# x's parts of two gates put into PSUM by ScalarE, update gate's products side by side in all steps

## The reference, cut to what matters

```python
vz = video @ C_z + b_z      # vr, vh likewise
xz = jnp.einsum('btd,de->bte', seq, W_z)   # xr, xh likewise
def step(h, xs):
    xzt, xrt, xht = xs
    z = jax.nn.sigmoid(xzt + h @ U_z + vz)
    r = jax.nn.sigmoid(xrt + h @ U_r + vr)
    hh = jnp.tanh(xht + r * h @ U + vh)
    h_new = (1.0 - z) * h + z * hh
    return (h_new, h_new)
```

## Time and profile before

| | |
|---|---|
| median of three runs | 1515.9 us |
| span of the profiled execution | 1513.4 us |
| the profiled execution's own time | not given; the median is 2.5 us above its span |
| TensorE busy | 1503.4 us, 99% |
| VectorE busy | 1332.9 us, 88% |
| ScalarE busy | 1066.1 us, 70% |
| GpSimd busy | 309.1 us, 20% |
| granted TensorE clock | 1.000 in the mean over the span |
| recurrence, t = 1 to the last product | 551 to 1508 us |

### The profile page before, as it was taken

How to read it: one execution, slowest core, us unless ns; L and a number is a source line. 1 busy time by engine, 2 the same in 40 slices (tenths; PEclk the granted TensorE clock), 3 DMA queues, 4 the chain that set the end, 5 groups by cost and what they waited for, 6 DMA issues and landing times.

```text
span 1513.4 us, 58048 instructions
## 1 busy us (share of the span) xinstructions
PE 1503.4 (99%) x24698; PEld 1177.8 (78%) x24698; DVE 1332.9 (88%) x2928; ACT 1066.1 (70%) x2481; POOL 309.1 (20%) x333
## 2 busy tenths in 40 slices
PE   9999999999999999999999999999999999999998
PEld 7874444444444467779999999999999999999998
DVE  7999999999999889888888888888888888877787
ACT  7989999999999833656666666566666666656333
POOL 1100112111110014322222222222222222222222
PEclk9999999999999999999999999999999999999999
DMA  5156465565649978533333333333333333320000
GB/s 198 35 158 189 94 194 139 136 157 145 176 89 143 148 112 82 74 51 23 49 21 49 48 21 49 45 24 49 21 48 47 20 48 30 39 41 4 31 32 31
DMA packets 544979, 116.86 MB, mean 77 GB/s; under 512 B 520144, under 2 KB 527056, under 8 KB 536016
## 3 DMA queue, kind: packets, MB, share of 16 engines
q1 hardware_dynamic: 537424, 82.21, 31.2%
q0 software_dynamic: 7008, 30.41, 10.9%
q10 hardware_dynamic: 288, 0.52, 0.1%
HBM read 66.47 MB, written 33.55 MB: 66 GB/s over the span
## 4 chain that ended last, share of the span: by engine, by line
PE 97%; DVE 2%; issue 1%; ACT 1%; DMA 0%; DVEq 0%
PE ps L1458 33%; PE ps L1560 22%; PE ps L1523 22%; PE ps L1572 12%; PE ps L1544 5%; PE ps L1476 2%; DVE ST L1303 0%; PE ps L1425 0%; DMA AR<-in_w1f 0%; PE ps L1489 0%; DVE RL L1338 0%; DVE AR L1270 0%; DVE HL L1382 0%; DVE ST L1308 0%; DVE ST L1389 0%
## 5 line engine op out<-in xcount | busy, mean ns | idle before, releaser
L1458 PE MATMUL ps<-XH,WH 128*128 128x512 f16 x1872 | 404.7, 379 | 0.0
L1458 PEld LDWEIGHTS ps<-XH,WH 128*128 128x128 f16 x1872 | 182.9, 98 | 220.2 <-issue 0.3
L1560 PE MATMUL ps<-HL,U 128*128 128x64 f16 x8016 | 275.5, 193 | 2.0 <-DVE HL L1382 1.7
L1560 PEld LDWEIGHTS ps<-HL,U 128*128 128x128 f16 x8016 | 259.2, 98 | 8.5 <-issue 3.5
L1675 POOL TENSOR_TENSOR ST<-ST 128x256 f32<-128x256 f32 x127 | 107.9, 849 | 460.5 <-ACT ST L869 460.5
L847 ACT ACTIVATE ST<-ST 128x128 f32<-128x128 f32 x254 | 71.9, 310 | 169.5 <-DVE ST L1303 169.5
L1572 PE MATMUL ps<-HL,U 128*128 128x64 f16 x4064 | 163.2, 194 | 0.0
L1303 DVE SCALAR_TENSOR_TENSOR ST<-ps,dn,AR 128x128 f32<-128x128 f32 (+1 forms) x320 | 108.6, 372 | 46.8 <-PE ps L1572 44.2
L1303 DVE SCALAR_TENSOR_TENSOR ST<-ps,dn,XP 128x128 f32<-128x128 f32 x315 | 107.4, 372 | 41.2 <-PE ps L1572 38.9
L1572 PEld LDWEIGHTS ps<-HL,U 128*128 128x128 f16 x4064 | 138.6, 98 | 0.1
L1560 PEld LDWEIGHTS ps<-RL,U 128*128 128x128 f16 x3952 | 131.9, 98 | 6.0 <-issue 0.9
(11 more groups left out here) (201 smaller groups left out, 2976.4 us busy)
## 6 DMA issues: line engine op xcount, KB each, us to landing
x_scratch<-AR SPq DMA_DIRECT2D x16, 1024.0 KB, 5.3
AR<-in_x POOLq DMA_DIRECT2D x15, 1024.0 KB, 8.1
AR<-HB POOLq DMA_DIRECT2D x11, 1024.0 KB, 7.0
raw<-x_scratch SPq DMA_DIRECT2D x88, 128.0 KB, 4.5
out_y<-raw SPq DMA_DIRECT2D x11, 1024.0 KB, 4.6
raw<-in_x SPq DMA_DIRECT2D x10, 1024.0 KB, 7.4
ST<-in_x SPq DMA_DIRECT2D x5, 1024.0 KB, 7.3
out_y<-AR SPq DMA_DIRECT2D x4, 1024.0 KB, 4.3
```

Of the source, the lines that this page charges most:

```text
L1458: op = pe.matmul(ps[b][:, :], v[:, g, wp, k, e * P:(e + 1) * P], y[:, xp, k, :], start=n == 0, stop=n == 11)
L1560: pe.matmul(ps[b][:, col:col + B], U[:, g, uh, k, e * P:(e + 1) * P], S[:, k, 0], start=opens, stop=False, skip_group_check=True)
```

## The change

It does three things.

1. **Two gates get x's part ahead of their products.** `held(t, g)` is true for R in steps 2 to 127 and for C in steps 2 to 119. In such a step ScalarE has put x's part, times a factor (`uh`), into the gate's two banks with one instruction (`put_x`, 256 elements), before the gate's first product; that product then doesn't open the bank anew but adds to what is there. VectorE's `add_x` falls away, and ScalarE's sigmoid and tanh read the bank, with the factor `dn` as their scale. R's put for step t+1 stands in ScalarE's program behind the f16 copy of r*h in step t; C's stands at the end of step t, behind the splitting of later x. TensorE waits for the puts (`s_put`) where it waited for the adds. In the first eight steps of C this also ends its being joint.
2. **Z is joint in all steps.** `is_joint` is `g == 0`. VectorE's add for Z is then two instructions, the second waiting for the first.
3. Three one-column factors `uh` are computed by VectorE in step 0; the eight banks are one tensor, so that one instruction can write two of them. Some semaphores are merged.

```diff
-JOINT = TC
+HELD_FROM, HELD_TO = 2, 15 * 8
...
         def is_joint(t, g):
-            return g != 1 and t < JOINT
+            return g == 0
+
+        def held(t, g):
+            return g == 1 and t >= HELD_FROM or g == 2 and HELD_FROM <= t < HELD_TO
...
+            def put_x(t, g):
+                j, tt = divmod(t, TC)
...
+                else:
+                    act.wait_ge(s_xp, xp_ready(t, g))
+                    if by_seven(j):
+                        act.wait_ge(s_xa, xa_count[turn(j, g, 4)])
...
+                    act.wait_ge(s_r if g == 1 else s_hh, 2 * (t - 1) + (0 if g == 1 else 2))
+                first = (R if g == 1 else C)[0]
+                banks = PS[:, first * 512:(first + 2) * 512].rearrange("p (h n) -> p h n", h=2)[:, :, 0:2 * B]
+                x = XP[j % 2][:, g].rearrange("p (h e) n -> p h e n", h=2)[:, :, :, tt * B:(tt + 1) * B]
+                act.activation(banks.rearrange("p h (e b) -> p h e b", e=2), x, ACT.Copy, scale=uh[:, g:g + 1]).then_inc(s_put[g], 1)
...
                     for h in range(2):
-                        act.wait_ge(s_pr, 2 * u + h + 1)
-                        act.activation(two(rg, h), two(rg, h), ACT.Sigmoid).then_inc(s_r, 1)
+                        if held(t, 1):
+                            act.wait_ge(s_R, 2 * u + h + 1)
+                            act.activation(two(rg, h), held_sums(R[h]), ACT.Sigmoid, scale=dn[:, scale(4)]).then_inc(s_r, 1)
...
+                    if t + 1 < T and held(t + 1, 1):
+                        put_x(t + 1, 1)
...
+                if t and t + 1 < T and held(t + 1, 2):
+                    put_x(t + 1, 2)
...
-                for h in range(2):
+                for h in range(0 if held(t, 1) else 2):
                     dve.wait_ge(s_R, 2 * u + h + 1)
                     add_x(t, rg, R[h], 1, (2 * h, 2 * h + 1), None, s_pr, 2 * u + h + 1)
...
-                                opens = kk == 0 and k == 0 and uh == int(joint) and (e % 2 == 0 if banks[0] != banks[1] else e == 0)
+                                opens = not held(t, g) and kk == 0 and k == 0 and half == int(joint) and (e % 2 == 0 if banks[0] != banks[1] else e == 0)
...
-                else:
-                    pe.wait_ge(s_pr, 2 * u)
+                elif held(t, 1):
+                    pe.wait_ge(s_put[1], puts(t, 1))
...
-                if u:
-                    pe.wait_ge(s_pc, 2 * u)
+                if held(t, 2):
+                    pe.wait_ge(s_put[2], puts(t, 2))
+                elif u:
+                    pe.wait_ge(s_hh, 2 * t)
```

More of the change, by code:

```diff
@@ L120, in build @@
         hhi, hlo, rhi, rlo = HL[:, :, 0], HL[:, :, 1], RL[:, :, 0], RL[:, :, 1]
-        ps = [ctx.enter_context(nc.psum_tensor(f"ps{i}", [P, 512], F32)) for i in range(8)]
+        PS = ctx.enter_context(nc.psum_tensor("ps", [P, 8 * 512], F32))[:, :]
+        ps = [PS[:, i * 512:(i + 1) * 512] for i in range(8)]
         W1F, W1I, W1H, UZ, UR, UH, CR, CZ, WR, WZ, CH, WH = range(12)
@@ L246, in build @@
         s_R, s_Z, s_C = sem("R"), sem("Z"), sem("C")
-        s_pr, s_zh, s_pz, s_ch, s_pc = (sem(n) for n in ("prer_", "z_high", "prez_", "c_high", "preh_"))
+        s_put = {1: sem("x_in_R"), 2: sem("x_in_C")}
+        s_pr, s_zh, s_pz, s_pc = (sem(n) for n in ("prer_", "z_high", "prez_", "preh_"))
         s_r, s_rhi, s_rf, s_rlo = (sem(n) for n in ("r", "rhi", "rf_", "rlo"))
@@ L387, in is_joint, with puts, sums_by_dve @@
         def is_joint(t, g):
-            return g != 1 and t < JOINT
+            return g == 0
+        def held(t, g):
+            return g == 1 and t >= HELD_FROM or g == 2 and HELD_FROM <= t < HELD_TO
+        def puts(t, g):
+            return sum(held(n, g) for n in range(t + 1))
+        def sums_by_dve(t, g):
+            return sum(not held(n, g) for n in range(1, t + 1))
         def halved_by_act(t):
@@ L731, in put_dv @@
                 put(i, DV[:, turns[i][1]], s_predv)
+            def put_x(t, g):
+                j, tt = divmod(t, TC)
+                if puts(t, g) == 1:
+                    act.wait_ge(s_ux1, 4)
+                if j == 0:
+                    act.wait_ge(s_xpa, KT * (W2_ORDER.index(g) + 1))
+                    act.wait_ge(s_xpb, KT * (B_ORDER.index(g) + 1))
+                else:
+                    act.wait_ge(s_xp, xp_ready(t, g))
+                    if by_seven(j):
+                        act.wait_ge(s_xa, xa_count[turn(j, g, 4)])
+                if t == HELD_FROM:
+                    act.wait_ge(s_pr if g == 1 else s_pc, 2 * (t - 1))
+                else:
+                    act.wait_ge(s_r if g == 1 else s_hh, 2 * (t - 1) + (0 if g == 1 else 2))
[3 more added lines that the diff above has]
+                act.activation(banks.rearrange("p h (e b) -> p h e b", e=2), x, ACT.Copy, scale=uh[:, g:g + 1]).then_inc(s_put[g], 1)
             def sigmoids(q):
@@ L845, in _ @@
                     for h in range(2):
-                        act.wait_ge(s_pr, 2 * u + h + 1)
-                        act.activation(two(rg, h), two(rg, h), ACT.Sigmoid).then_inc(s_r, 1)
+                        if held(t, 1):
+                            act.wait_ge(s_R, 2 * u + h + 1)
+                            act.activation(two(rg, h), held_sums(R[h]), ACT.Sigmoid, scale=dn[:, scale(4)]).then_inc(s_r, 1)
+                        else:
+                            act.wait_ge(s_pr, 2 * u + h + 1)
+                            act.activation(two(rg, h), two(rg, h), ACT.Sigmoid).then_inc(s_r, 1)
                     before = done_second(t - 1)
@@ L874, in _ @@
                     for h in range(2):
-                        act.wait_ge(s_pc, 2 * u + h + 1)
-                        act.activation(two(hg, h), two(hg, h), ACT.Tanh).then_inc(s_hh, 1)
+                        if held(t, 2):
+                            act.wait_ge(s_C, 2 * u + h + 1)
+                            act.activation(two(hg, h), held_sums(C[h]), ACT.Tanh, scale=dn[:, scale(5)]).then_inc(s_hh, 1)
+                        else:
+                            act.wait_ge(s_pc, 2 * sums_by_dve(t, 2) - 1 + h)
+                            act.activation(two(hg, h), two(hg, h), ACT.Tanh).then_inc(s_hh, 1)
                     if halved_by_act(t):
@@ L1326, in _ @@
                     dve.tensor_tensor(hlo, Hn, hhi, ALU.subtract).then_inc(s_hlo, 1)
+                    for g in range(3):
+                        dve.wait_ge(s_up, scaled(3 + g))
+                        dve.tensor_scalar(uh[:, g:g + 1], up[:, scale(3 + g)], HS, None, ALU.mult).then_inc(s_ux1, 1)
                     evacuate_first(t)
@@ L1358, in _ @@
                         sw_lo(i, t - SUMS[i] - 5)
-                for h in range(2):
+                for h in range(0 if held(t, 2) else 2):
                     dve.wait_ge(s_C, 2 * u + h + 1)
-                    add_x(t, hg, C[h], 2, (2 * h, 2 * h + 1), s_ch, s_pc, 2 * u + h + 1)
+                    add_x(t, hg, C[h], 2, (2 * h, 2 * h + 1), None, s_pc, 2 * u + h + 1)
                 for h in range(2):
@@ L1555, in recurrent_first @@
                         for k in (2 * kk, 2 * kk + 1):
-                            for uh in ((1,) if joint else (0, 1)):
+                            for half in ((1,) if joint else (0, 1)):
                                 b = banks[e // 2]
                                 col = (e if banks[0] == banks[1] else e % 2) * per
-                                opens = kk == 0 and k == 0 and uh == int(joint) and (e % 2 == 0 if banks[0] != banks[1] else e == 0)
-                                pe.matmul(ps[b][:, col:col + B], U[:, g, uh, k, e * P:(e + 1) * P], S[:, k, 0],
+                                opens = not held(t, g) and kk == 0 and k == 0 and half == int(joint) and (e % 2 == 0 if banks[0] != banks[1] else e == 0)
+                                pe.matmul(ps[b][:, col:col + B], U[:, g, half, k, e * P:(e + 1) * P], S[:, k, 0],
                                           start=opens, stop=False, skip_group_check=True)
```

13 lines of the change are left out of this document (8 added, 5 removed).

## The result

The changed kernel takes 1511.58 us (median of 7 runs, 1509.92 to 1512.01), the kernel before beside it 1515.13 us (7 runs, 1514.93 to 1516.64): a ratio of 0.9974, 95% interval 0.9965 to 0.9984. That is 0.26% faster in the median, with 0.2% inside the interval. 1511.1 was forecast, from 1515.9. The profiled execution has a span of 1509.8 us and takes 1511.58, so 1.8 us lie around the span.

The account below looks back on a forecast made before the run. TensorE's own list was taken to bound nearly all steps. Terms -4.80 + 0.28 - 0.43 + 0.15 summed to -4.80 us, taking 1515.9 to 1511.1 us, with a range of 1509.8 to 1513.6.

Parts of the forecast that it names:

- inner range of 1510.0 to 1512.0: Whole kernel's time in us if unknown costs leave TensorE unhindered: early waits 0.43, tail 0.36, 0.002 in reading the 0.040.
- Z joint, -4.80: TensorE, steps 8 to 127: joint products save 0.040 us in each of 120 steps, all on the path.
- Rival C: TensorE: 128-column products cost more among 256-column fill; gain lost at 2.5 ns more each, 1515.9 us; chance 0.02.
- C not joint +0.28: TensorE, steps 1 to 7: C no longer joint costs 0.040 us in each of 7 steps.
- early waits -0.43: First steps: TensorE's waits for r*h's low part go as VectorE loses adds; bounds 0 and -0.43 us.
- The puts at nothing: ScalarE: two puts of 0.48 us each per step, neither late, so no cost on the path; ScalarE at about 77%.
- rival D: Puts: TensorE overwrites them or waits; a wait needs R's put 2 us later; chance 0.02 with others.
- The low part of r*h, room 0.29: VectorE, steps 8 to 111: Z's second add cuts room from 0.80 to 0.29 us; waiting begins at 0.06.
- Rival A: r*h's low part too late for TensorE in 104 steps, from 0.23 us further delay; 1523.6 us at 0.35; chance 0.07.
- Rival B: ScalarE late in 13 chunk changes or ten early steps, 0.2 us each: 2 to 3 us, 1513 to 1514; chance 0.09.
- The end, +0.15, bounds 0 and 0.51: Last step: Z's double add precedes C's adds and Z's sigmoids; R's 0.38 us earlier covers part of 0.51.

Follow-up runs that it names:

- Experiment 2: Kernel before the change with Z joint in all steps and no puts, C joint in steps 0 to 7: 1518.49 us, ratio 1.0026.
- experiment 6: Changed kernel with C's put moved behind the splitting of the weights on ScalarE: 1511.30 us, ratio 0.9973.
- Experiments 3: Changed kernel with 7 unused products of 512 columns filling TensorE's idleness ahead of step 127: 1509.97 us, ratio 0.9967.
- 7: Changed kernel with Z not joint in the last two steps, 126 and 127: 1509.67 us, ratio 0.9961.
- 8: Changed kernel with C's put behind the splits, Z not joint in steps 126 and 127, and 7 unused products ahead of step 127: 1508.53 us, ratio 0.9957.
- experiments 4: Changed kernel with an unused 256-element VectorE instruction ahead of r*h's low part in steps 8 to 111: 1525.9 us, ratio 1.0072.
- 5: Changed kernel with an unused 64-element VectorE instruction ahead of r*h's low part in steps 8 to 111: one run of 1510.59 us.
- experiments 1: Changed kernel with the puts kept but Z joint only in steps 1 to 7, as before the change: 1514.18 us, ratio 0.9995.

## Why the prediction was right

It named 1511.1 us, 1511.58 came, and the sign, the main term and its mechanism held. The difference of the medians, though, is 3.55 us and not 4.80. The time came so near because the base was too high as well: the kernel before measured 1515.13 beside the change, not 1515.9 (1.8 us lie around a span, not 2.5). From 1515.13 the sum would have given 1510.33, 1.25 us too low. (The inner range of 1510.0 to 1512.0 is not its own terms either: they give 1510.7 to 1512.1.)

- **Z joint, -4.80.** Right: 0.040 us in each step, 3.76 in the 94 from 18 to 111. Rival C is out: the 128-column products stay 0.89 / 16 = 56 ns apart amid 256-column fill. The Trainium skill, "TensorE: Matmul & The Clock Gate", section Back-to-back issue gap, has 56 ns for this as its figure without weight loads and 81 ns for a stream with them; each product here has a load of its own, and the measurement decides for 56.
- **C not joint +0.28, early waits -0.43.** Right for steps 1 to 7: -0.16 against -0.15.
- **The puts at nothing.** Right for the path: a put is 0.464 us in the mean (0.48 taken), ScalarE is busy for 75% of steps 40 to 47 (77% taken), and the puts alone change nothing that can be told. TensorE waits for none of the puts in the profile, so nothing of rival D is seen (its wait would have needed R's put nearly 4 us later by the earlier trace rows, not 2). I had costed them by what they take. Experiment 2 shows what they give: without them Z joint loses.
- **The low part of r*h, room 0.29.** Right in 102 of the 104 steps: 0.26 to 0.28. In steps 8 and 9 it was late by 0.14 each. Rival A's limit of 0.06 held in the dose test, with 0.21 to spare in place of 0.23. At 0.33 of delay the kernel was at 1525.9; the rival had 1523.6 for 0.35.
- **Rival B** came true in two steps, 0.22 + 0.30 us, of the ten for which it was priced. It was the put that waits for an emptied bank, with splits behind it, as the rival had said; experiment 6 takes 0.39 of the 0.52 away. Half of it reaches TensorE as rival A's late low part. The sum had no term for it.
- **The end, +0.15, bounds 0 and 0.51.** This is the term that failed. Its own part was a matter of size: TensorE idles 0.23 us longer (Z's second add now stands ahead of C's adds, with the emptying of a bank as before, and they start 0.90 after C's second group, before 0.67). But I took the work of step 127 as unaltered, and it ran in part at the lower clock: 1.5 us more from R to the end, outside my bounds. In experiment 6's profile, with the same end but a clock of 1.00, it was 9.8 us, so 1.3 of the 1.5 is the clock. Experiments 3, 7 and 8, without the long idle stretch, end 9.6 to 9.9 us after R.
- **Not in the sum:** the 0.40 in steps 16 and 17 that went with the puts, the stalls of 0.67 in step 113, an accident of 0.29 in the profile of before. I had named them only as possible gains for the range's edge. They pay for most of what the end lost, so the nearness of 1511.1 to 1511.58 is in part luck.

By rows, from R of step 1 to R of step 127: -4.76 for Z (119 steps), -0.16, +0.46 for steps 8 and 9, -0.69 for steps 16 and 17, -0.67, +0.23, in all -5.59 (952.87 to 947.28).

## What to carry to other kernels

Where one engine is the path, price a change by that engine's own list and then look for the covers that it thins; a dose test (a bit more work in the thin place) tells how deep a cover is. A change may consist of a part that earns and a part that only makes room for it, and trying each alone may reject both. Where an edit lengthens an idle stretch of TensorE (here by 0.23 us, to 1.89), price the work behind it at the lower clock as well, and where an instruction that waits on a third engine is put into an in-order queue, read what stands behind it.

## What the hardware did that I had not expected

- After 1.89 to 1.90 us without a product TensorE ran at a granted clock of 0.50 (1.2 GHz) in part of step 127, in five of six profiles with this stretch (the changed kernel three times, experiments 4 and 5). In the profile of experiment 6 it stayed at 1.00 with the same 1.90, and in that of experiment 2 with 2.35. After 1.66 (before, twice) and 1.43 (experiments 1 and 7) it stayed at 1.00. So a long idle stretch is not sufficient, and so few cases show no limit; what else decides is open.
- The clock also fell between 5 and 10 us in three of the thirteen profiles (0.75, 0.78 and 0.86: the changed kernel twice, experiment 6). There TensorE had waited 1.05 to 1.53 us for x's first block, in the other ten 0.70 to 0.91, and R of step 1 starts latest, at 551.30 to 551.54. But it still moves between 549.64 and 551.06 over the other ten, of before and of altered kernels alike, and the cause of that is open. The whole spread, 1.9 us, is about half of what the change is worth.
- In the recurrence TensorE pauses in some executions without a releaser, idle for 0.24 to 0.61 us. The one in step 113 stood at the same product in both profiles of before, others came once (at 1169.47 us in the second profile of the changed kernel, none so long in its first and third; at 984.00 and 1507.34 us in experiment 1). I have no cause for them.
